# Who normalises the later tokens of a Mamba scan: GpSimd's eight subtractions and products become ScalarE activations with a bias that GpSimd prepares

## What is computed

```python
def _layernorm(x, axis=-1, eps=1e-05):
    m = jnp.mean(x, axis=axis, keepdims=True)
    v = jnp.var(x, axis=axis, keepdims=True)
    return (x - m) / jnp.sqrt(v + eps)
...
proj = hidden_states @ W_in.T            # hidden_states = _layernorm(x)
z, xBC, dt = ...                         # 4096 z, 4096 x, 128 B, 128 C, 64 dt channels
xBC = silu(conv4(xBC) + conv_b)
y = scan over 256 positions, 64 heads of 64, state 128, decays exp(dt * A)
g = (y + D * x) * silu(z)
out = (g * rsqrt(mean(g * g) + EPS)) * norm_w @ W_out.T
```

## Time and profile before

| | us |
|---|---|
| three runs | 1664.67, 1667.51, 1669.19 |
| median of the runs | 1667.51 |
| the profiled execution's own time | 1667.24 |
| its span | 1665.5 |
| mean granted clock of TensorE | 0.986 of full speed |
| TensorE / VectorE / ScalarE / GpSimd busy | 1593.5 / 1246.0 / 1212.6 / 817.8 |
| eight `normalise` instructions on GpSimd (L349) | shortest 1.215, middle 1.964, longest 2.709 each |

### The profile page before, as it was taken

How to read it: one execution, slowest core, us unless ns; L and a number is a source line. 1 busy time by engine, 2 the same in 40 slices (tenths; PEclk the granted TensorE clock), 3 DMA queues, 4 the chain that set the end, 5 groups by cost and what they waited for, 6 DMA issues and landing times. The chain is left out here.

```text
span 1665.5 us, 29161 instructions
## 1 busy us (share of the span) xinstructions
PE 1593.5 (96%) x9876; PEld 1282.4 (77%) x9876; DVE 1246.0 (75%) x1954; ACT 1212.6 (73%) x2533; POOL 817.8 (49%) x648
## 2 busy tenths in 40 slices
PE   4998999999999999999999999999969999999999
PEld 3776777777777777777777667877748889999888
DVE  6899999999898999998899656766566534333355
ACT  5999999999999999999999566766624334444331
POOL 5587676575555555555565422211124563335460
PEclk8999999999999999999999999999979999999999
DMA  7545455344444444464442100000214333222231
GB/s 283 179 167 190 169 186 174 134 157 163 158 152 153 152 159 165 161 246 153 167 163 89 57 1 14 13 14 26 95 73 171 130 105 112 93 92 93 78 101 51
DMA packets 76239, 209.85 MB, mean 126 GB/s; under 512 B 9152, under 2 KB 32960, under 8 KB 74304
## 3 DMA queue, kind: packets, MB, share of 16 engines
q1 hardware_dynamic: 70432, 181.90, 31.9%
q0 software_dynamic: 5664, 26.09, 4.5%
HBM read 170.99 MB, written 36.96 MB: 125 GB/s over the span
## 5 line engine op out<-in xcount | busy, mean ns | idle before, releaser
L1006 PE MATMUL banks<-pair_hi,m_wxz 128*128 128x512 f32 x1024 | 353.6, 406 | 3.9 <-DVE pair_lo L659 2.3
L734 DVE SCALAR_TENSOR_TENSOR m_xc<-banks,m_cw,m_xc 128x510 f32<-128x510 f32 (+2 forms) x384 | 285.6, 744 | 14.4 <-ACT m_xc L493 4.3
L376 POOL TENSOR_TENSOR m_mat<-m_mat,m_cb_off 128x512 f32<-128x512 f32 x128 | 166.4, 1300 | 210.6 <-DVE m_mat L746 201.4
L507 ACT ACTIVATE m_mat<-m_a_all,m_cum 128x256 f32<-128x256 f32 x512 | 262.1, 512 | 1.4 <-PE m_ps_y L1047 1.4
L1063 PE MATMUL m_ps_out<-m_won,m_gT 128*128 128x256 f32 x1024 | 242.5, 379 | 3.6 <-POOL m_gT L385 2.2
L1006 PEld LDWEIGHTS banks<-pair_hi,m_wxz 128*128 128x128 f32 x1024 | 194.7, 190 | 42.9 <-issue 2.7
L385 POOL TENSOR_TENSOR m_gT<-m_gy,m_zs 128x512 f32<-128x512 f32 x128 | 166.8, 1303 | 120.1 <-DVE m_gy L776 120.1
L1063 PEld LDWEIGHTS m_ps_out<-m_won,m_gT 128*128 128x128 f32 x1024 | 191.7, 189 | 34.3 <-POOL m_gT L385 3.9
L510 ACT ACTIVATE m_mat<-m_a_all,m_cum 128x128 f32<-128x128 f32 x512 | 206.7, 404 | 0.0
L1006 PE MATMUL banks<-pair_lo,m_wxz 128*128 128x512 f32 x512 | 201.5, 394 | 0.0
L1047 PE MATMUL m_ps_y<-m_mat,m_xdt 128*64 128x256 f32 (+1 forms) x2048 | 194.7, 332 | 0.0
(11 more groups left out here) (347 smaller groups left out, 3440.1 us busy)
## 6 DMA issues: line engine op xcount, KB each, us to landing
m_a_all<-a_by_head SPq DMA_DIRECT2D x128, 512.0 KB, 4.0
m_wxz<-w_split SPq DMA_DIRECT2D x96, 512.0 KB
w_split<-m_wxz SPq DMA_DIRECT2D x32, 512.0 KB, 3.0
raw<-in_w_gate_up POOLq DMA_DIRECT2D x9, 1280.0 KB, 6.6
raw<-in_w_xz SPq DMA_DIRECT2D x32, 256.0 KB, 4.1
raw<-in_w_down POOLq DMA_DIRECT2D x9, 640.0 KB, 7.7
x_sorted<-f_gT_hi SPq DMA_DIRECT2D x1, 4992.0 KB, 16.2
f_xg<-x_sorted SPq DMA_DIRECT2D x39, 128.0 KB, 2.5
```

Of the source, the lines that this page charges most:

```text
L376: pool.tensor_tensor(off, off, cb_off[:, g * BG:(g + 1) * BG, :].rearrange("p b t -> p (b t)").unsqueeze(1) .broadcast_to([P, HPT, BG * P] ...
L507: act.activation(first_rows(u, h, b), a_all[u][:, h, b * SEQ:(b + 1) * SEQ].rearrange("p (j t) -> p j t", t=P), ACT.Relu, bias=cum[:, t, h ...
L734: dve.scalar_tensor_tensor(out=out[:, :, k:], in0=ps[:, :, 0:SEQ - k], scalar=cw[:, c, TAPS - 1 - k:TAPS - k], in1=out[:, :, k:], op0=ALU. ...
L1006: last = pe.matmul(ps[:, :], w, a, start=m == 0, stop=m == len(terms) - 1)
```

## The change

ScalarE gets a `normalise` that writes the same tiles of `xn` as `Identity(rstd * x + off_mean)`: two tiles at j = 10 and two at j = 12 of the first and of the second group, at the head of its `prepare_next`, that is behind `tanh_z` and ahead of `w_high` and `decays`. GpSimd no longer normalises; at j = 5 it forms, beside `rstd`, `off_mean = -mean * rstd` for the four tiles of a group, two instructions of 128 x 4. A tensor of 128 x 16 and two semaphores are added.

```diff
+        off_mean = sb("off_mean", [P, NT])
...
+        ln_minus, ln_off = sem("ln_minus"), sem("ln_off")
...
-            def normalise(n):
-                pool.wait_ge(ln_rstd, n // TPG + 1)
-                pool.wait_ge(xT_ready, n - TPG - (TPG if n < EARLY + TPG else 0) + 1)
-                pool.tensor_scalar(xn[:, xn_slot(n), :], xres[:, n, :], mv[:, n, 0:1], rstd[:, n:n + 1],
-                                   ALU.subtract, ALU.mult).then_inc(normed_late, 1)
+            def ln_offset(g):
+                ts = slice(g * TPG, (g + 1) * TPG)
+                pool.tensor_scalar(off_mean[:, ts], mv[:, ts, 0], -1.0, 0.0, ALU.mult, ALU.add).then_inc(ln_minus, 1)
+                pool.wait_ge(ln_rstd, g + 1)
+                pool.wait_ge(ln_minus, g - 1)
+                pool.tensor_tensor(off_mean[:, ts], off_mean[:, ts], rstd[:, ts], ALU.mult).then_inc(ln_off, 1)
...
                 if g < NG - 2:
                     if j == 5:
                         ln_root(g + 2)
-                    if 7 <= j < 7 + TPG:
-                        normalise((g + 2) * TPG + j - 7)
+                        ln_offset(g + 2)
...
+            def normalise(n):
+                act.wait_ge(ln_off, n // TPG - 1)
+                act.wait_ge(xT_ready, n - TPG - (TPG if n < EARLY + TPG else 0) + 1)
+                act.activation(xn[:, xn_slot(n), :], xres[:, n, :], ACT.Identity, bias=off_mean[:, n:n + 1],
+                               scale=rstd[:, n:n + 1]).then_inc(normed_late, 1)
+
             def prepare_next(n):
                 h, j = n // NCT + 1, n % NCT
+                if j in (10, 12) and h + 1 < NG:
+                    for n in range(2):
+                        normalise((h + 1) * TPG + n + (2 if j == 12 else 0))
```

## The result

The kernel after takes 1671.89 us (median of 7 executions, 1670.15 to 1674.5), the kernel before 1667.87 in the same runs (7, 1664.67 to 1669.36): 4.0 us more, a ratio of 1.0026 [1.0014, 1.0038]. That is under the 0.3% that I had set as the bound of "no change", but the interval shows that it is a loss, and the time lies 0.3 us above the range given, 1664.6 to 1671.6. The profiled execution took 1672.70 us, 5.46 more than that of before.

The account below looks back on a forecast made before the run. VectorE was taken to set the pace in the first group, TensorE in the second. First group -0.5 + 0.5 + 0 = 0, second +1.15, on the profiled 1667.24: 1668.4 us, no measurable change; range 1664.6 to 1671.6.

Parts of the forecast that it names:

- What does not move: Whole kernel: no DMA and no order on TensorE, VectorE or SyncE changes; moved tokens and later instructions have slack.
- An activation: ScalarE, j = 10 and 12: one normalise 0.59 us long, costing 0.48 back to back, a pair 0.96.
- The second group, +1.15: ScalarE's pairs cost 1.92 us, less 0.64 and 0.13 of room: 1.15 late at j = 14, passed to VectorE and TensorE.
- The small instructions at j = 5: GpSimd: 0.28 us each, delaying L396 in the first group so VectorE loses 0.5 us; nothing lost in the second.
- the swap that they cause at 102 us: First group: VectorE's L712 goes ahead of GpSimd's L396 and is short; L746 behind it waits, 0.5 us lost.
- L349's going: GpSimd's normalising removed: VectorE's steps gain 0.17 us in three of four first-group steps, 0.5 us; nothing in the second.
- ScalarE's two pairs in the first group: 1.92 us of activations against 4.6 us idle, covered by VectorE's hold-up: costs nothing, 1.92 us if that cover is gone.
- B: First group: every VectorE hold-up beside an L349 is given back, 3.2 us over three steps: 1664.0 us; chance 0.08.
- The one step under the 7.3 us: Sign that every hold-up is given back: VectorE's steps at j = 8 to 11 of the first group under 7.3 us.
- C: ScalarE, both groups, j = 10 and 12: no wait absorbs anything, all eight activations cost 5.3 us: 1672.5; chance 0.09.
- A: ScalarE's waits absorb all its added work and GpSimd's relief stays, a gain of 0.5 us: 1666.7; chance 0.16.
- D: ScalarE loads a function table for Identity, costing more than all the rest; 0.05 together with anything not thought of.

Follow-up runs that it names:

- e4: Kernel before with 64 unused bytes ahead of the weights m_wxz and 64 behind, so the rest lies 128 bytes later: 1671.00 us, +3.3.
- e1: Kernel before with an unused 64-byte pad where the change puts off_mean, no instruction changed: 1672.01 us, +4.3.
- e2: Kernel after with off_mean allocated last, so every other buffer lies where it lay before: 1668.77 us, +1.0 against the kernel before.
- e5: Kernel before with 96 unused bytes ahead of the output projection's won and 32 behind, the projection weights moved by 128: 1670.28 us, +1.6.
- e11: Kernel before with 96 unused bytes ahead of f_room, the expert layers' weights, putting them on a multiple of 256: 1667.59 us, -2.6.
- e8: e2 with the second group's later pair of activations split over j = 21 and 25: 1666.75 us, -2.0 against the kernel before.

## Why the prediction was right in its parts and wrong in its sum

**The step that failed** is in "What does not move": "No DMA, and no order on TensorE, VectorE or SyncE, changes." The sentence is true, and I took an order that stays for a duration that stays. The diff adds a tensor, and I gave its 64 bytes no term, neither a price nor a bound. It is worth 3.3 (e4) to 4.3 us (e1). By the groups, after against e2 loses 1.1 in the second and 1.7 in the third, and after against before 1.5 in the fourth: 4.3 us, which is 0.053 us in each of some 80 steps that TensorE sets. In the second group, up to j = 16, ScalarE's delay hides the place's, 0.5 us by then in e1: TensorE's mark there is 1.21 us later in after, measured from j = 5, and 1.18 in e2. In the first group, where VectorE sets the pace, the place costs 0.3 at most (e1, e4). With the moved work as e2 has it, -0.5 and +1.1, that makes the scan's 4.9 us. Added to the forecast, the place alone would give 1671.7 to 1672.7, beside a median of 1671.89.

**The moved work** was priced rightly in the loss and at half in the gain:

- An activation is 0.590 to 0.608 us long (0.59 said) and a pair takes ScalarE 354.08 - 353.10 = 0.98 (0.96).
- The second group, +1.15: e2 has +1.1, and 1.18 at TensorE's mark of j = 16. The path is the one described: the wait at j = 10 took up a part of the first pair, j = 12 had no room, VectorE waited for L495 and TensorE for VectorE. It began sooner than written: in e2 VectorE waits at j = 11 already, 0.35 us, which is the 0.98 of the first pair less the 0.64 of room, and 0.63 at j = 12.
- The small instructions at j = 5 take 0.20 us each, not 0.28; the swap that they cause at 102 us came as told. The mark of VectorE behind it is at 105.16 us for 104.41, 0.2 of which was there from the start and 0.1 at the mark ahead: 0.45 us, and 0.44 in e2 (0.5 said).
- L349's going was the term mis-sized in the moved work. It gave 0.22 to 0.24 us in three of the four steps beside an L349 and 0.40 in the fourth, 1.1 us, where I had said 0.17 in three, 0.5. In after and in e2 alike that leaves 0.45 - 1.1 = -0.65 between VectorE's marks before and behind; the whole group is 0.5 shorter, where I had 0. (In one execution a group with the orders of before can be 1 us shorter by itself, as in e5 and e11; there it comes at j = 4, ahead of all this.)
- ScalarE's two pairs in the first group, nothing: behind the fourth of these steps VectorE's marks keep their lead of 0.5 to 0.6 us to the group's end.

**The rivals.** B, every hold-up given back, is refuted: steps of 7.40 us and not 6.5, since L399 goes on holding VectorE (1.68 us for 0.74 at 117 us, begun 0.15 us behind L399). The one step under the 7.3 us that I had named as its sign is the fourth, 7.13. The Trainium skill (SBUF — State Buffer, § SBUF: two separate sides) has the lock held for a whole instruction by whoever starts first. The two rows agree; that the hold-up passes to the next instruction when one sharer goes is what this trace adds. C, in which no wait absorbs anything, gave 1672.5 and so nearly the time measured, by a wrong road: e2 shows that in the second group the waits did absorb 0.8 of two pairs' 1.96 us, and in the first all of it. A time that fits is no proof of its case. A and D did not occur.

The same section of the Trainium skill gives TensorE two independent read ports, one for the streamed operand and one for loading weights, and says that it never waits on anyone. Taken to mean that it is all one where its operands lie, the runs are against it: e1, with nothing changed but the places, is 4.3 us slower.

## What to carry to other kernels

A new tensor is part of a change: it moves all that is allocated behind it, and where TensorE sets the pace, the distance of the loaded from the streamed operand is worth a look (in this projection best at a multiple of 256 bytes; the output projection did not care). Allocate small additions last, or test an unchanged kernel with a pad of the same size. Beside the count and order of a bound engine's instructions, compare the cadence of one of its repeated blocks before and after: 0.8% of a step, in some 80 steps, is most of what this change lost. And extra work on an engine goes where that engine waits, step by step: the same two activations cost 0.9 us more at j = 12 than at j = 21 and 25 (the second group of e2 and of e8, one execution each).

## What the hardware showed that I had not expected

- TensorE's matmuls of 128 x 512 in float32r, back to back, follow each other after 0.2295 us if the distance of their two operands in a partition is a multiple of 256 bytes, and after 0.2333 to 0.2336 with 64 bytes more; the step is 6.553 with 32 and 6.554 with 128 more. In the expert layers, a block of 60 goes from 14.0 us (160 and 224 bytes off) to 13.6 (0). The output projection's float32 matmuls of 256 columns last the same 0.378 to 0.379 us at 224, 32 and 0 bytes. Other distances, types and shapes were not tried; what in the memory does it, no run shows.
- A hold-up between VectorE and GpSimd can change the instruction that bears it (L746 before, L723 after) with most of the step's length kept (7.62 to 7.40 us).
- In the expert layers TensorE has a pause near 1312 us that comes and goes from one execution to the next, nothing in before, 2.1 us in e1 (whose code is that of before, but for the places; it comes there at 1321 us) and 2.96 in e11. In e11 the granted clock falls to 0.53 behind it, and matmuls are 0.63 us long for 0.39. Profiled executions differ by it and by the wait for weights near 750 us, so the verdicts above rest on medians and on steps, not on the span of a profile:

```profile
1315.43 0.79 PE L2482 MATMUL f_gu<-pair_hi,f_room 128*128 128x512 f32 x1 [2.96 <-issue]
```
